# Adaptive-norm transformer block with a hand-made order of five engines: all pieces placed anew by a table of begin times

## What is computed

```python
mod = (silu(c) @ wmod).reshape(8, 6, 1, 256)       # sa, ca, ga, sb, cb, gb
h = layernorm(x) * (1 + ca) + sa
q, k, v = einsum(h.reshape(B, T, 16, 16), w_q | w_k | w_v)   # head-wise 16x16
q, k = rope(q), rope(k)
x = x + ga * (softmax(causal(q @ k.T / 16)) @ v)   # one head of width 256
h = layernorm(x) * (1 + cb) + sb
for l in range(2):
    q, k, v = split(shift_token(h) @ wqkv[l])      # 8 heads of 64
    q, k = xpos(l2norm(q) * qs, l2norm(k) * ks)
    h = h + windowed_attention(q, k, v, window=128) @ wo[l]
    n = layernorm(shift_token(h))
    a, g = split(n @ w1[l] + b1[l])                # 2 x 682 columns
    h = h + (a * gelu(g)) @ w2[l] + b2[l]
x = x + gb * h
```

## Time and profile before

| | before |
|---|---|
| median of three runs | 3000.75 us (2998.53 to 3004.02) |
| the profiled execution | 3003.69 us, its span 3001.9 us |
| TensorE matmuls busy | 2734.4 us (91%), 21452 instructions |
| VectorE busy | 2489.0 us (83%), 7195 instructions |
| ScalarE busy | 1793.8 us (60%), 4181 instructions |
| GpSimd busy | 1343.1 us (45%), 949 instructions |
| DMA, share of 16 engines over the span | 5.4%, 46.29 MB |
| granted TensorE clock, mean | 0.986 of full speed |

### The profile page before, as it was taken

How to read it: one execution, slowest core, us unless ns; L and a number is a source line. 1 busy time by engine, 2 the same in 40 slices (tenths; PEclk the granted TensorE clock), 3 DMA queues, 4 the chain that set the end, 5 groups by cost and what they waited for, 6 DMA issues and landing times.

```text
span 3001.9 us, 63211 instructions
## 1 busy us (share of the span) xinstructions
PE 2734.4 (91%) x21452; PEld 1918.9 (64%) x21452; DVE 2489.0 (83%) x7195; ACT 1793.8 (60%) x4181; POOL 1343.1 (45%) x949
## 2 busy tenths in 40 slices
PE   2399998999899998899989999899998999899997
PEld 2167675676666676666756767567765667666675
DVE  3489888888889887898878988889887988889895
ACT  2147673577646776376754767457764677637674
POOL 1145443545335454455534544344543545435552
PEclk9799999999999999999999999999999999999999
DMA  5100001000000000000010000100000000000000
GB/s 157 34 2 6 7 5 36 3 6 4 22 21 5 5 7 24 15 5 5 8 30 9 6 4 8 36 3 5 5 22 20 5 5 7 24 15 5 5 8 18
DMA packets 57996, 46.29 MB, mean 15 GB/s; under 512 B 18466, under 2 KB 54988, under 8 KB 57556
## 3 DMA queue, kind: packets, MB, share of 16 engines
q1 hardware_dynamic: 53520, 35.14, 4.2%
q10 hardware_dynamic: 4164, 7.12, 0.7%
HBM read 25.42 MB, written 8.44 MB: 11 GB/s over the span
## 4 chain that ended last, share of the span: by engine, by line
PE 64%; DVE 12%; ACT 6%; POOL 5%; issue 5%; DMA 4%; DVEq 0%; ACTq 0%; POOLq 0%
PE ps L134 11%; PE ps L135 11%; PE ps L136 11%; PE ps L400 8%; PE ps L426 7%; PE ps L411 5%; PE ps L335 4%; DMA XS<-xu 4%; PE ps L386 2%; PE ps L354 2%; ACT ar_b L569 2%; PE ps L294 2%; DVE ar_b L796 2%; POOL small L907 1%; DVE ar_b L780 1%
## 5 line engine op out<-in xcount | busy, mean ns | idle before, releaser
L907 POOL TENSOR_TENSOR small<-small,neg_half 128x16 f32<-128x16 f32 x128 | 406.2, 3174 | 416.7 <-DVE small L743 414.9
L569 ACT ACTIVATE ar_b<-ar_b,small 128x256 f32<-128x256 f32 (+1 forms) x1024 | 492.9, 484 | 103.6 <-DVE small L780 100.9
L780 DVE CUSTOM_DVE_ANT_0 ar_b<-ps,mask_t,small 128x256 f32<-128x256 f32 (+1 forms) x1024 | 419.5, 462 | 28.3 <-PE ps L400 25.1
L911 POOL TENSOR_TENSOR ar_c<-ar_c 128x1024 f32<-128x1024 f32 x128 | 301.9, 2358 | 229.7 <-DVE ar_c L769 229.0
L796 DVE TENSOR_SCALAR ar_b<-ar_b,rsw 128x256 f32<-128x256 f32 (+1 forms) x1024 | 302.9, 359 | 9.2 <-DVE rsw L789 0.2
L242 POOL TENSOR_SCALAR stats<-stats 128x2 f32<-128x2 f32 x128 | 29.9, 234 | 596.5 <-DVE stats L828 259.0
L134 PE MATMUL ps<-wqkv_hi,ht_hi 128*128 128x512 f16 x768 | 292.0, 380 | 0.0
L135 PE MATMUL ps<-wqkv_lo,ht_hi 128*128 128x512 f16 x768 | 291.1, 379 | 0.0
L136 PE MATMUL ps<-wqkv_hi,ht_lo 128*128 128x512 f16 x768 | 291.1, 379 | 0.0
L400 PE MATMUL ps<-ar_a 64*128 64x128 f32 x3840 | 271.4, 285 | 15.6 <-ACT ar_a L559 15.6
L411 PE MATMUL ps<-id_f,ar_b 128*128 128x128 f32 x1920 | 269.9, 276 | 17.0 <-DVE ar_b L796 16.5
(11 more groups left out here) (170 smaller groups left out, 6669.2 us busy)
## 6 DMA issues: line engine op xcount, KB each, us to landing
xu<-in_L_attn_x_dram SPq DMA_DIRECT2D x32, 256.0 KB, 2.9
out_dram<-xu SPq DMA_DIRECT2D x64, 128.0 KB, 2.8
XS<-xu SPq DMA_DIRECT2D x128, 63.5 KB
ar_a<-in_L_ffn_wqkv_dram ACTq DMA_DIRECT2D x1, 3072.0 KB, 16.9
modb<-mod_rows SPq DMA_DIRECT2D x8, 384.0 KB, 5.5
XS<-xu SPq DMA_DIRECT2D x112, 0.5 KB
ar_a<-in_L_wmod_dram SPq DMA_DIRECT2D x1, 1536.0 KB, 7.6
xu<-in_L_ffn_w_dram SPq DMA_DIRECT2D x1, 1364.0 KB, 9.3
```

Source lines behind the costliest of these rows:

```text
L569: last = act.activation(pw, pw, ACT.Exp, bias=mnw[:, n % 2, h:h + 1], scale=-1.0, accum_out=smw[:, n % 2, h:h + 1])
L780: last = dve.tensor_tensor_reduce(out=PW[:, f, q, i, c:2 * P], in0=ps[:, bk, i * 256 + c:(i + 1) * 256], in1=mask_t[:, c:2 * P], scale=rin ...
L907: pool.tensor_tensor(rinv[:, n % 4, :], ssm[:, n % 2, :], neg_half[:, 0:16], ALU.pow).then_inc(s_rinv, 1)
L911: pool.tensor_tensor(M1[:, n % 2, :], M1[:, n % 2, :], M2, ALU.add).then_inc(s_add, 1)
```

## The change

`schedule()` no longer works out begin times from offsets. A table `BEGIN` holds one for every piece of a batch, by kind and engine, and a constant the distance from batch to batch, 339.26. The tables of offsets, `SHIFT` and the helper `in_batch` are gone. The numbers are all new; they were set so that VectorE's and GpSimd's operations that touch SBUF alone are placed with regard to each other. The pieces, their instructions, their waits and `plan_banks` are the same text. Only the table's two first kinds, the lines of the pieces that the prediction speaks of, and the code are shown:

```diff
-ATTN_TILE = [-0.64, 1.6, 21.99, 38.98, 48.92, 61.23, 67.63, 73.8]
-WIN_TILE = [5.24, 16.02, 29.76, 42.02, 55.85, 69.1, 82.37, 94.55]
...
-SHIFT = {("D", 0, 0): 8.86, ("D", 0, 1): -3.37, ("D", 0, 2): -5.63, ("D", 0, 3): 0.61, ("D", 1, 0): -5.8,
...
+PERIOD = 339.26
+BEGIN = {
+    ("D", "pe"): {(0, 0): 35.28, (0, 1): 54.32, (0, 2): 80.65, (0, 3): 87.25, (1, 0): 171.98, (1, 1): 195.1,
...
+    ("N", "pe"): {(0, 0): 120.75, (0, 1): 139.56, (0, 2): 180.71, (0, 3): 200.18, (1, 0): 275.43, (1, 1): 276.74,
+        (1, 2): 329.49, (1, 3): 334.15},
...
+    ("pj", "pe"): {0: -7.23, 1: -6.25, 2: 15.49, 3: 20.48, 4: 34.3, 5: 35.72, 6: 44.2, 7: 45.17},
...
 def schedule():
 
     made = []
-
-    def put(time, engine, *piece):
-        made.append((round(time + SHIFT.get(in_batch(piece), 0.0), 2), engine, piece))
...
+    for (k, engine), at in BEGIN.items():
+        for ids, time in at.items():
+            ids = ids if isinstance(ids, tuple) else (ids,)
+            for b in range(NB):
+                if k in BY_TILE:
+                    piece = (k, b * DEPTH * NT + ids[0], *ids[1:])
+                elif k in BY_LAYER:
+                    piece = (k, b * DEPTH + ids[0], *ids[1:])
+                else:
+                    piece = (k, b, *ids)
+                made.append((round(time + b * PERIOD, 2), engine, piece))
     made.sort()
     return ({e: [q for _, g, q in made if g == e] for e in ("sp", "pe", "act", "dve", "pool")},
             {q: time for time, _, q in made})
```

More of the change, by code:

```diff
@@ L932 @@
 BY_LAYER = ("D", "N", "Wg", "Wa", "dh", "dl", "nh", "nl", "ls", "lt", "lk", "ge", "us", "uh", "ul")
[L935 to L939, removed]
-ATTN_TILE = [-0.64, 1.6, 21.99, 38.98, 48.92, 61.23, 67.63, 73.8]
-WIN_TILE = [5.24, 16.02, 29.76, 42.02, 55.85, 69.1, 82.37, 94.55]
-MLP_BLOCK = [[48.18, 47.24, 50.71, 50.97, 55.45, 58.45], [45.14, 51.2, 51.64, 54.6, 56.44, 57.48]]
@@ L946 @@
[L946 to L954, removed]
@@ L955 @@
-PT_AT = (("pt", "pe", 8.59), ("pc", "dve", 17.24))
-LN2_AT = {"r2": ("pool", -7.05), "l2": ("dve", 34.65)}
-WIN_AT = {("xs",): ("sp", -39.35), ("E", 0): ("pe", -4.43), ("E", 1): ("pe", -3.81), ("ev", 1): ("act", -1.19),
[12 rows of a table removed]
-LN_AT = {"ls": ("dve", 41.15), "lt": ("pool", 41.52), "N": ("pe", 43.08), "nl": ("dve", 43.66), "nh": ("act", 44.91),
-         "lk": ("dve", 45.03)}
-D_AT = {"dh": ("act", -2.08), "D": ("pe", 3.83), "dl": ("dve", 6.88)}
-MLP_AT = {"ge": ("act", 0.33), "uh": ("act", 1.98), "us": ("dve", 2.27), "ul": ("pool", 8.19)}
@@ L974 @@
[L974 to L977 removed]
[234 rows of a table removed]
+PERIOD = 339.26
+BEGIN = {
[203 rows of a table added]
+}
 def schedule():
     made = []
[L1218 to L1274 removed]
```

50 lines of the change are left out of this document (removed), and 445 rows, old and new, of tables (BEGIN, SHIFT, WIN_AT).

## The result

The changed kernel takes 2896.8 us (median of four runs, 2895.4 to 2900.4), beside 3002.0 for the kernel before on the same chip (the three runs above and a fourth): a ratio of 0.965, 95% interval 0.964 to 0.967, and 105 us less. The forecast was 2860. The median lies at the very edge of the range, 0.2 us inside it; the mean of the four runs, 2897.4, is 0.4 outside.

The account below looks back on a forecast made before the run. Small TensorE waits behind chains of short operations, partly VectorE and GpSimd stopping each other, were blamed. Gains of 102.6 (six spacings), 15.6 (last) and 23.5 (batch 0), together 141.7 us, gave 2860 us, range 2840 to 2897.

Parts of the forecast that it names:

- L761 undisturbed: VectorE's L761 of tile 1 no longer runs under GpSimd's L911; 1.22 us undisturbed, against a 1.42 mean before.
- L636 at 0.9 for two: VectorE's L636 runs ahead of the L855 that starts GpSimd's L926: 0.9 us for two instead of 2.7.
- the power operation that stops nobody: GpSimd's L907 does not block VectorE, so the 20 or so pieces the table puts under it cost VectorE nothing.
- table loads count for nothing: ScalarE's table loads fall from 126 to 110, 2.6 us per batch, counted at nothing because TensorE's and VectorE's work covers it.
- L823's wait: VectorE's L823 waits for the shifted rows' DMA, 4.8 us per spacing before; forecast to stay near 5 us.
- slip of chip against table: Chip's spacing over the table's 339.26 us: 0.8 us taken, giving 340.1; bounds -2 and +7.3.
- one slow stretch more per batch: Clock rival: one more half-clock stretch per batch than planned, 1.7 us x 8, 2874 us; inside the plan-kept chance of 0.70.
- The last spacing: Last batch-to-batch distance, no next batch to share with: 4.4 us shorter than the others, 335.7, gain 15.6 us.
- Batch 0: First batch, first projection to end: from 384.8 to 361.3 us, gain 23.5 us.
- Collisions come back: Rival: GpSimd and VectorE stop each other again out of phase, 4 to 5 us per spacing, 2896 us; chance 0.20.
- held ports: Rival: two-input VectorE operations under GpSimd's L907 wait for its end, 20 us per spacing, 3025 us; chance 0.01.
- late rows: Rival: VectorE's L823 waits longer for shifted rows, holding work behind it; at 3 us each 3060 us; chance 0.02.

Follow-up runs that it names:

- The thin one: Changed kernel plus unused matmuls at three waits and a VectorE swap; second of three 512-column matmuls in E, Wg, Wa cut to 480 columns: 2872.6 us, ratio 0.9571.
- The L769 cut: Changed kernel plus unused matmuls at three waits and a VectorE swap; second L769 left out in every window but the first: 2883.1 us.
- the version with the swap: Changed kernel plus unused matmuls ahead of three TensorE waits, and L837/L839 moved ahead of window 4's L769 on VectorE: 2880.7 us, ratio 0.9596.
- the one place tried alone: Changed kernel with L636 of the second pair of tiles put back behind the L855 that starts GpSimd's L926: 2893.8 us, ratio 0.9643.

## Why the prediction was off

**What bounds it, and the parts.** The frame held: setup and tail all but unchanged, the change works on the spacing. The forecast took 141.7 us off the profiled execution, 108.3 came: 26.8 of the missing 33.4 in the six spacings (344.57 for 340.1), 6.5 in the last, 1.1 in batch 0; the setup gave 1.0. L761 undisturbed, L636 at 0.9 for two and L386 without its listed wait came as said. So did the power operation that stops nobody: in the two runs where GpSimd does hardly anything but powers, VectorE's lines have their undisturbed lengths. That table loads count for nothing was not tried by itself; ScalarE's share of the last chain fell from 6 to 4%. L823's wait was forecast near 5 us and is 2.4.

**The step that failed is the slip of chip against table**: 0.8 us per spacing, taken "nearest to rows" between -2 and +7.3. It measured 344.57 - 339.26 = 5.3, inside the bounds and far from the choice. Its parts:

- *Drift, 3.3.* The undisturbed spacing is 342.53. Set beside the table piece by piece in batch 3, TensorE is late by 0.34 us at 28 us behind the first projection, 1.1 at 94, 2.0 at 182, 3.1 at 327. On TensorE itself the slots are nearly right: six matmuls of Wg or Wa take 1.30 us where the table has 1.29 and 1.30 in turn, and over the half-layer of them from 153 to 170 us the lag grows by 0.03. It grows in some thirty steps of 0.05 to 0.24 us, which make 2.6 of the 3.3. Slots that are long against the table are found on VectorE: two L769 fill 1.21 us for 1.19, four L837 and L839 1.02 for 1.00 (both in the rows of batch 2 above: 921.95 to 923.16, and on to 924.18). And VectorE is late first: from 154 to 173 us its lag goes from 1.8 to 2.0 while TensorE's stays below 1.8, and by 194 us TensorE is 2.2 late too. A place where TensorE takes such a lag over, at 94 us (TensorE, then GpSimd):

```profile
1233.35 0.38 PE L136 MATMUL ps<-wqkv_hi,ht_lo 128*128 128x512 f16 x1
1233.70 0.98 PE L386 MATMUL ps<-id_f,ar_c 128*128 128x128 f32 x7
```

```profile
1232.61 1.04 POOL L917 TENSOR_TENSOR ar_c<-ar_c,small 128x512 f32<-128x512 f32 x1
```

  L386 begins 0.35 us behind the matmul ahead of it, where a slot of 512 columns is 0.216, and just behind the end of L917 at 1233.65. L917 is 1.2 us late against the table (93.38 us behind the first projection for 92.17), as is the L769 ahead of it, and TensorE was 0.95 late before. The matmul ahead is listed with 0.38, so no wait shows.

  The prediction had looked for slots that were short against the rows, found the pair L719, L723 and the four L837 and L839, and took these for the whole. In a plan without slack the rest adds up. That much the trace shows; the cuts don't turn it into shares. The thin one (2.5 us less work, 1.5 less in the spacing) has TensorE's chain pass most of a cut on. The L769 cut brought TensorE's lag at 130 us from 1.4 to 0.8 or 0.9, and at 153 us it was 1.7 to 1.8 again, so a further chain held the time there; which, was not followed. Nor was it what makes the early steps, up to 0.8 at 52 us.
- *Clock, about 1.7.* A rival had it, with "one slow stretch more per batch", 14 us; it was 15 in all, measured by taking the stretches away. The prediction ruled it inside the range and left it out of the sum ("clock stretches included"), though the table has gaps of 2.1 and 1.6 us at the very place. It also read the earlier trace rows as once per spacing behind the wait of 2.92. The number is near enough, eight in the steady part, but only two of them are behind that wait; the others are behind waits of 1.15 and 1.4 us.
- *The one-off, 0.3 on the mean*: one stop of 2.0 us in six spacings.

**The last spacing** was to be 4.4 shorter than the others. It is 2.4 shorter, with three lengths of 3.4 us at half clock in it (the row 2859.40:2866.20 and one from 2883.3 on). With one of them left, in the version with the swap, it is 339.1 against 342.7, 3.6 shorter. So the term was right in kind and at most 0.8 too large; the clock took the rest.

**Batch 0** was forecast at 361.3 and took 362.4.

**The rivals.** "Collisions come back" gave a spacing of 344.6 and 2896 us, both nearly the measured numbers, and was wrong about the cause: without VectorE's stops the new order takes the same 2897.6. A time that matches a rival's is not yet that rival. The diagnosis of before had the same flaw the other way round: it put 22 us of stretched operations per spacing beside the 34 of waits and let them look like cause and effect; VectorE's share of them, taken away in the old order, was worth 1.3. The rivals of held ports and of late rows did not happen. What the new order gained is for the greater part TensorE's waits, 19.6 us to 10.7 per spacing. The weight loads of L400 stand less too (their idle time over the run, before and after, 61.1 and 37.2):

```profile
L400 PEld LDWEIGHTS ps<-ar_a 64*128 64x128 f32 x3840 | 232.8, 189 | 61.1 <-issue 36.5 <-ACT ar_a L559 24.6
```

```profile
L400 PEld LDWEIGHTS ps<-ar_a 64*128 64x128 f32 x3840 | 225.8, 187 | 37.2 <-issue 19.5 <-ACT ar_a L559 17.8
```

**What stays open.** Which of the many moves brings how much: the one place tried alone was worth nothing, and running the old order of GpSimd within the new table wasn't tried, nor the new order with the banks of the old. Whether the gain is the order's or in part that of the PSUM banks, which the same numbers hand out, is therefore not shown. What GpSimd's standing behind VectorE costs was not measured, nor which engine's slots make how much of the drift. Nor is it settled which waits make the clock fall.

## What to carry to other kernels

A timetable that engines follow in order is a good forecast of the time, but only after its slots are compared with the trace to three digits on every engine of the chain: steps of 0.05 to 0.24 us, some of which no list of waits shows, were over half of this miss, and few of them were TensorE's own slots. Price an engine's stretched operations by taking the stretching away in the old order, not by adding up their excess. And when the waits of TensorE get few, look at which of them the clock falls behind, over all batches and not in one: unused matmuls ahead of three waits were worth 15 us here, more than VectorE's stops in the old order (10), and the same trick with only some of the waits covered made the old order slower.

## What the hardware showed beyond that

- The granted clock halved behind waits of TensorE of only 1.7 and 2.0 us in the new order, and of 1.15 and 1.4 us in the old one, for 3.4 or 6.8 us at a time, in some batches and not in others of the same order. A wait of 2.92 us at L294 had a stretch behind it in two batches and none in five.
- An operation of VectorE with one SBUF input (L839, 128 columns) stood for the whole of an L911, 2.38 us for 0.34, when it began 0.16 us behind it.
- TensorE stood for 0.1 us or so without a wait in the list: L386 begins 0.35 us behind a matmul of 512 columns instead of 0.216, and 0.05 behind the end of the L917 that makes its input.
- Powers of GpSimd on a few columns left VectorE at its undisturbed lengths: with them in place of its long operations, L761 took 1.22 us and L796 0.35 on the mean. The powers themselves took 3.15 us in the old order and 2.94 in the new one.
- In the new order VectorE was busy 5 us less per spacing without its stops, and the time did not move.
